# The second attention's value remainders: VectorE, one step later, in place of GpSimd

## The reference, cut to what matters

```python
y_dca, y_main = y[:, -16:, :], y[:, :-16, :]          # y is the context
kv_dca = (y_dca @ Wkv_dca + bkv_dca).reshape(b, 16, 2, 16, 32)
k_dca, v_dca = _ln(kv_dca[:, :, 0], kn_dca_w, kn_dca_b), kv_dca[:, :, 1]
kv = concatenate([y_main @ Wk + bk, y_main @ Wv + bv], -1)
k, v = _ln(kv[..., :32], kn_w, kn_b), kv[..., 32:]     # 16 heads of 32
```

## Time and profile before

| | us |
|---|---|
| median of 3 runs | 2778.57 |
| lowest and highest of them | 2777.77, 2778.73 |
| the profiled execution's own time | 2780.01 |
| its span, from the first to the last instruction | 2778.2 |

### The profile page before, as it was taken

The page is one execution under the profiler, slowest core; times in us unless marked ns, Lnnn a source line. Parts: engine busy times, 40 slices in busy tenths (PEclk is TensorE's granted clock), DMA queues, the critical chain, the costliest instruction groups (busy, mean ns, idle before and its releaser), DMA issues.

```text
span 2778.2 us, 46215 instructions
## 1 busy us (share of the span) xinstructions
PE 2405.0 (87%) x14828; PEld 1993.5 (72%) x14828; DVE 1705.3 (61%) x3850; ACT 1487.6 (54%) x3093; POOL 1098.9 (40%) x1556
## 2 busy tenths in 40 slices
PE   5999999999985798988898574999997589889878
PEld 3778878788774688888887453999996467667733
DVE  2555555555565466666666573566555488778856
ACT  3644444444453556666666435444442388667745
POOL 0322222322320344444444247677775455444400
PEclk9999999999987799999999787999999799999989
DMA  3300000000032000000000327676675652332000
GB/s 130 118 22 8 19 11 19 8 19 11 8 121 91 12 20 19 19 19 19 19 0 19 106 98 227 190 201 188 185 193 125 160 147 62 79 73 57 1 4 31
DMA packets 147526, 198.38 MB, mean 71 GB/s; under 512 B 21925, under 2 KB 85797, under 8 KB 147045
## 3 DMA queue, kind: packets, MB, share of 16 engines
q1 hardware_dynamic: 131672, 160.70, 19.3%
q0 software_dynamic: 10992, 25.96, 4.4%
q10 hardware_dynamic: 4768, 10.62, 1.2%
HBM read 151.09 MB, written 46.15 MB: 71 GB/s over the span
## 4 chain that ended last, share of the span: by engine, by line
PE 69%; DVE 10%; ACT 7%; issue 7%; DMA 3%; POOL 3%; DVEq 0%; SPq 0%; ACTq 0%; POOLq 0%
PE pair L2271 8%; PE pair L655 7%; PE pair L1199 5%; PE pair L1249 4%; PE pair L683 4%; PE pair L2758 4%; PE pair L616 4%; PE pair L641 3%; PE pair L2289 3%; PE pair L1271 3%; PE pair L2741 3%; PE pair L672 2%; PE pair L1233 2%; PE pair L2770 2%; PE pair L622 2%
## 5 line engine op out<-in xcount | busy, mean ns | idle before, releaser
L531 ACT ACTIVATE x_p<-x_p,x_least 128x1024 f32<-128x1024 f32 x128 | 147.1, 1149 | 267.1 <-DVE x_least L482 267.1
L587 POOL TENSOR_TENSOR x_carry<-x_rtotal 128x1 f32<-128x1 f32 x128 | 24.7, 193 | 573.4 <-DVE x_rtotal L459 573.4
L466 DVE TENSOR_TENSOR x_pT<-pair,x_pT 128x512 fp32r<-128x512 f32 x256 | 164.4, 684 | 126.5 <-ACT x_pT L552 126.5
L2271 PE MATMUL pair<-m_h,e_w 128*128 128x320 f32 x1536 | 230.5, 310 | 1.1 <-DVE m_h L2186 1.1
L2271 PEld LDWEIGHTS pair<-m_h,e_w 128*128 128x128 f32 x1536 | 229.0, 190 | 2.7 <-issue 1.5
L655 PE MATMUL pair<-x_pT,x_v 128*128 128x256 f32 x1536 | 214.0, 297 | 15.6 <-DVE x_pT L466 15.6
L655 PEld LDWEIGHTS pair<-x_pT,x_v 128*128 128x128 f32 x1536 | 198.4, 198 | 32.9 <-issue 22.7
L1111 ACT ACTIVATE s_p<-s_p,s_least 128x128 f32<-128x128 f32 (+3 forms) x256 | 143.6, 561 | 123.2 <-DVE s_least L1021 123.1
L683 PE MATMUL pair<-x_kT,x_qT 128*128 128x512 f32 x768 | 207.0, 404 | 0.0
L2666 DVE TENSOR_REDUCE z_most<-pair 128x1 f32<-128x1008 f32 x128 | 154.0, 1203 | 82.7 <-PE pair L2780 51.2
L1249 PE MATMUL pair<-s_pT,s_v 128*128 128x256 f32 (+1 forms) x1152 | 158.8, 284 | 47.5 <-DVE s_pT L998 47.5
(11 more groups left out here) (350 smaller groups left out, 6113.6 us busy)
## 6 DMA issues: line engine op xcount, KB each, us to landing
e_raw<-in_L_ffn_w SPq DMA_DIRECT2D x48, 1024.0 KB, 5.7
z_kS<-z_k SPq DMA_DIRECT2D x24, 512.0 KB, 9.6
hslot<-in_L_ffn_w ACTq DMA_DIRECT2D x16, 512.0 KB, 3.6
hT_x<-in_L_ffn_w SPq DMA_DIRECT2D x16, 512.0 KB, 5.1
z_v<-z_vst SPq DMA_DIRECT2D x16, 512.0 KB, 3.0
z_vS<-z_v SPq DMA_DIRECT2D x8, 960.0 KB, 5.0
z_qS<-z_q SPq DMA_DIRECT2D x24, 256.0 KB, 4.3
s_wraw<-in_L_ffn_wq SPq DMA_DIRECT2D x9, 512.0 KB, 4.3
```

The costliest lines, as they stand in the source:

```text
L466: dve.tensor_tensor(pT[1][:, keys, q * P:(q + 1) * P], TR[j][:, :].rearrange("p (k n) -> p k n", n=P), pT[0][:, keys, q * P:(q + 1) * P].b ...
L531: act.activation(p[n][:, :], p[n][:, :], ACT.Exp, scale=-1.0, bias=least[:, n:n + 1], accum_out=total[:, n:n + 1]).then_inc(s_ex, 1)
L2271: mm = pe.matmul(GU[m % 2][:, j * BANK:j * BANK + CAP], w[x0][:, c, m * P:(m + 1) * P], XS[s][x1][:, c, :], start=(n == 0 and c == 0), sto ...
```

## The change: what it does

The subtraction that gives the low part of the values is taken out of GpSimd's order and put into VectorE's. GpSimd did it for unit s in step s; VectorE does it for unit s-1 at the end of step s, behind that unit's reciprocal. All operands, tiles, slots and semaphore counts stay, and so do the orders of ScalarE, TensorE and SyncE.

```diff
@@ vector(dve, s), the part for u = s - 1 @@
                     dve.wait_ge(s_dev, u + 1)
                     dve.reciprocal(rdev[:, u * NH:(u + 1) * NH], dev[:, u * NH:(u + 1) * NH]).then_inc(s_rd, 1)
+                    if units[u][0] == "k":
+                        n = u - B
+                        hi, lo = values_parts(n % 2)
+                        dve.wait_ge(s_vh, n + 1)
+                        dve.tensor_tensor(lo, vt[n % 2][:, :, :], hi.bitcast(F32), ALU.subtract).then_inc(s_vl, 1)
@@ gpsimd(pool) @@
-                    u = s
-                    if u < len(units) and units[u][0] == "k":
-                        n = u - B
-                        hi, lo = values_parts(n % 2)
-                        pool.wait_ge(s_vh, n + 1)
-                        pool.tensor_tensor(lo, vt[n % 2][:, :, :], hi.bitcast(F32), ALU.subtract).then_inc(s_vl, 1)
```

## The result

The changed kernel takes 2788.99 us in the median of six runs (2785.29 to 2791.21), the kernel before 2777.64 in six on the same chip (2774.98 to 2778.73). The ratio is 1.0041 with a 95% interval of 1.0031 to 1.0051: slower by 11.4 us, between 8.6 and 14.2. The forecast was 2791.2, +12.6.

A forecast was written before the change was run, and what follows sets the result against it. In the changed stretch GpSimd's 3.5 us a step was the bound, the values' two-slot loop just under it. Nine periods +9.1, front +3.5, tail 0: 12.6 on 2780.0, less 1.4 for the median, 2791.2; range 2786.5 to 2798.

The forecast's parts named there:

- The loop: Low part, its store, high part, root, reciprocal: one step left in place of two, so 4.80 us a step.
- Nine periods: From the reciprocal of unit 7 to that of unit 16: 43.2 us against 34.1, +9.1.
- the rival: The experiments' other theory: VectorE's 0.63 us more a step, and VectorE and GpSimd holding each other up, are the cost.
- The front: The steps ahead of the nine periods, steps 3 to 7: together +3.5 us, with bounds 1.5 and 5.
- step 5: A subtraction in front of the top-4 work, right behind the reciprocal: +0.6 us.
- step 6: The gates: four small operations move later and fall into GpSimd's held L1603, perhaps L1618; +1.5 us, between 0.6 and 1.8.
- step 7: The casts and L1789: +0.6 us for the subtraction and as much back from GpSimd's removed instruction, 0.
- The tail: From the reciprocal of unit 16 to the last landing, over the keys' stores: 0, between -1 and +1.5 us.
- the order of SyncE's queue: If ScalarE waits for the keys' slots too, up to 1 us more in each of the last four steps: 2795.
- The relief: Rival: the store's landing does not hold ScalarE, and the transfers set 3.3 us a step; -4.4, 2776.3; chance 0.09.
- The subtraction was held: Rival: GpSimd's L1618 holds VectorE's subtraction each time, up to 1.73 us; nine periods +18.8, 2801; chance 0.04.
- TensorE's clock: Rival: in the long steps the clock falls to the lower level, a step about 6.4 us; +23.5, 2806; chance 0.04.

The follow-up runs named there:

- gpsimd_late: The kernel before, with GpSimd still making the low part of the values, but of unit s-1 in step s; nine periods 59.92 us, whole 2811.57 us, ratio 1.0135.
- same_step: The changed kernel with VectorE's subtraction not a step later, but of unit s at the end of step s; nine periods 33.43 us, whole 2776.12 us.
- late_three: The changed kernel with three slots for the values' tile in place of two; nine periods 34.01 us, whole 2780.98 us, ratio to before 1.0019.
- half_store: The changed kernel with half of each values' tile stored, 256 KB in place of 512; nine periods 37.82 us, whole 2791.41 us in one run.
- split_late: The changed kernel, but GpSimd keeps the subtraction for units up to 7; VectorE has it, a step later, from unit 8; nine periods 42.71 us, whole 2785.68.
- late_sync_later: The changed kernel with SyncE storing the values of unit s-1, no longer of unit s, in step s; tail 17.26 us, whole 2790.55 us.
- split_same: The kernel before, with VectorE making the low part from unit 8 on in the same step, GpSimd up to unit 7; nine periods 33.24 us, ratio 0.9994.
- before_three: The kernel before with three slots for the values' tile in place of two; nine periods 34.81 us, whole 2775.38 us, ratio 1.0000.

## Why the prediction was right

**The loop.** It was the term that decided, and it holds in each of its parts: the subtraction at 0.63 (0.66 in the forecast), a store of 3.0, 0.86 from the high part's start to the reciprocal (1673.08 to 1673.94; 0.87 in the forecast), 4.74 to 4.80 a step where the forecast had 4.80 (one step with a store of 3.49 took 5.26). Nine periods cost +9.23, forecast +9.1. gpsimd_late (lateness without the engine), same_step (the engine without lateness), late_three (the slot given back) and half_store (the term made shorter) each move it as this account says and as the rival doesn't. gpsimd_late also measures the loop that the kernel before goes round in two steps: 6.66 us, where the prediction had about 6.7.

The estimate of 3.2 us for the store, which the prediction takes from the Trainium skill, DMA: Bandwidth & Descriptors (Anatomy of one DMA), rests on a fit that the page gives for transfers issued by GpSimd. These stores are issued by SyncE, so their 3.0 us don't speak for or against it, and the sum did without it.

**The front.** +2.18 against +3.5. Step by step, from the reciprocal of unit 0: TensorE's L1724 (L1723 after) starts 0.99 later (forecast 1.4, for the store landed in 3.0 and not up to 3.6) and then takes 7.67 in place of 8.10; step 5 +0.54 (0.6); step 6 +1.64 (1.5); step 7 -0.53 (0). The 0.43 that these 24 matmuls gave back can't be put down to the change: they took 8.14 in split_late, 8.21 in late_three and 7.28 in same_step. Step 6 is the holding up that was read from L1522: a multiplication of 128x128 elements stood behind GpSimd's held L1608 (L1603 before), and the last of the four, L1779 (L1780 before), behind L1617:

```profile
1648.80 0.63 DVE L1534 TENSOR_TENSOR z_vst<-z_vt,z_vst 128x512 fp32r<-128x512 f32 x1
1649.35 1.13 DVE L1775 TENSOR_TENSOR r_logit<-r_logit,r_chosen 128x128 f32<-128x128 f32 x1
...
1651.07 0.83 DVE L1779 TENSOR_TENSOR m_gate<-r_logit,r_rtotal 128x128 f32<-128x128 f32 x1
```

In step 7 one of GpSimd's two instructions went away and gave back more than the subtraction took: L1789 fell from 1.16 us to 0.33. The instructions of the two engines hold each other up in both places, once as a cost and once as a gain.

**The tail.** This is the term that was off: 0 was taken, with 1.5 as the upper bound, and it cost 1.76. The forecast said "nothing" of SyncE's moved queue. That was right for the slots in the middle of the pipeline, and wrong at its end. SyncE in order of time, after:

```profile
1708.62 0.37 SPq L1466 DMA_DIRECT2D z_v<-z_vst  x1
1709.04 0.51 SPq L1473 DMA_DIRECT2D z_k<-z_sthi  x1
1709.59 1.04 SPq L1474 DMA_DIRECT2D z_k<-z_stlo  x1
1711.30 0.37 SPq L1466 DMA_DIRECT2D z_v<-z_vst  x1
1711.71 0.72 SPq L1473 DMA_DIRECT2D z_k<-z_sthi  x1
1712.48 1.33 SPq L1474 DMA_DIRECT2D z_k<-z_stlo  x1
```

Six stores, 2 MB, are issued within 4 us. ScalarE's L1590 then waited 2.70, 1.95 and 0.41 us for keys' slots in its last three steps, 5.1 in all. In the kernel before, the same three (L1585) had waited 1.08 for GpSimd and 2.21 and 0.49 for keys' slots, 3.8 in all, so the keys' slots were a limit at the end already, and 1.3 us came on top. late_sync_later takes 1.5 us of the tail away. The rival that the prediction called the order of SyncE's queue did come true, at less than its upper bound.

**How much was luck.** The loop's +9.23 against +9.1 was not luck in the main, for each of its parts was measured as written; without the one store of 3.49 it would have been +8.7. That the sum fits so well was luck: the front was put 1.3 us too high and the tail 1.8 too low, and the two errors left 12.6 against 13.17. The medians, at 11.4, hold differences between executions as well.

**The rivals.** The relief was real on GpSimd (32.45 to 23.49 us busy) and brought nothing; where the loop is opened it is worth 0.7 to 0.9 us in nine periods, not the 4.4 that the rival had. Its 3.3 us a step were right for the middle periods of split_same (3.2 to 3.4), but it had them for all nine, while the first and last, with the longer bias add, stay at 4.4 and their neighbours at 3.8 and 4.0. The subtraction was held only once, the last time, 1.54 us. TensorE's clock stayed at 0.93 in the nine periods.

## What to carry to other kernels

Moving an instruction a step later is a change of buffering: for each slot that it frees, count the steps between the free and the next use, and put the store's landing on that path. An engine that is busy for 95% of a stretch may hide a loop that is nearly as long, so that relief on the engine is worth only the gap to the next limit (here 0.7 to 0.9 us in nine periods for 9 us of work), while a step taken from the loop costs in full (9.2). Before taking work from a bound engine, ask what has two steps now and one afterwards. If one must go later, a third slot gave back the cost in the loop here, though not that at the front and in the tail; where the loop had its two steps, it gave next to nothing.

## What the runs showed of the hardware

- SyncE was busy for 0.37 us with issuing a values' store of 512 KB, and for 0.51 with a keys' low store issued 0.4 us behind the high one (late_sync_later). As the third issued within a microsecond, the same low store took 1.04 and 1.33 in the rows of the tail above. So the engine that issues can itself be held; by what, no run here shows.
- Two-operand VectorE instructions in SBUF and GpSimd's instructions held each other up: with the subtraction just ahead, GpSimd's normalising took 1.36 or 1.37 in nearly every step where it had taken 1.05, a multiplication of 128x128 elements behind it took 1.13 where it had taken 0.23, and L1524 of before_three, against three of GpSimd's instructions, 3.21. The Trainium skill, GPSIMD Engine Reference (Key points), says that the two share their SBUF interfaces and contend where VectorE has two SBUF inputs; the trace agrees, with the sizes given here.
